# Segment scan of the second block: the key–value update in one round, the output weight held in TensorE, the q feature on VectorE, and a new order on four engines

## The reference

```python
def step(carry, inp):                      # one segment of 32 tokens, all sequences and heads
    mem, z = carry
    q_s, k_s, v_s, qn_s, kn_s = inp        # q, k with rotary embedding; qn, kn without
    scores = jnp.einsum('bhnd,bhmd->bhnm', q_s, k_s) * SCALE
    scores = jnp.where(mask, scores, -jnp.inf)
    sdpa = jnp.einsum('bhnm,bhmd->bhnd', jax.nn.softmax(scores, axis=-1), v_s)
    sq = elu1(qn_s)                        # elu(x) + 1
    num = jnp.einsum('bhnk,bhkv->bhnv', sq, mem)
    den = jnp.einsum('bhnk,bhk->bhn', sq, z)[..., None]
    out = beta * num / (den + 1e-06) + (1.0 - beta) * sdpa
    sk = elu1(kn_s)
    prev_v = jnp.einsum('bhnk,bhkv->bhnv', sk, mem) / jnp.einsum('bhnk,bhk->bhn', sk, z)[..., None]
    mem = mem + jnp.einsum('bhnk,bhnv->bhkv', sk, v_s - prev_v)
    z = z + sk.sum(axis=2)
    return ((mem, z), out)
...
out = o @ w_out                            # o: 16 heads of 64, w_out 1024 x 128; plus the fp8 linear layer of x
```

## Time and profile before

| | |
|---|---|
| median of 3 runs | 3249.21 us (3244.59 to 3251.42) |
| the profiled execution | 3244.0 us |
| its span in the trace | 3242.3 us |
| the scan's first projection to the end | about 1785 to 3242 us |
| PE, DVE, ACT, POOL busy over the span | 86%, 77%, 59%, 58% |

### The profile page before, as it was taken

The page is one execution under the profiler, slowest core; times in us unless marked ns, Lnnn a source line. Parts: engine busy times, 40 slices in busy tenths (PEclk is TensorE's granted clock), DMA queues, the critical chain, the costliest instruction groups (busy, mean ns, idle before and its releaser), DMA issues. The chain is left out here.

```text
span 3242.3 us, 132427 instructions
## 1 busy us (share of the span) xinstructions
PE 2791.2 (86%) x55025; PEld 1639.4 (51%) x55025; DVE 2481.5 (77%) x7469; ACT 1921.3 (59%) x3909; POOL 1895.3 (58%) x2112
## 2 busy tenths in 40 slices
PE   5675999999999999974250899999999999999998
PEld 2332333333333333354130567766676677776666
DVE  3566888888888888856715687887888788778876
ACT  4565788888888888831000555555555555555543
POOL 4664122222222222231053899989999999999986
PEclk9877899999999999986565899999999999999999
DMA  3557433333433334175023000000000000000000
GB/s 112 192 184 240 97 92 98 91 89 94 100 93 91 92 93 102 38 238 149 0 41 87 10 11 11 11 7 8 11 11 11 11 11 11 11 11 11 4 7 11
DMA packets 179276, 210.15 MB, mean 65 GB/s; under 512 B 28592, under 2 KB 140144, under 8 KB 178416
## 3 DMA queue, kind: packets, MB, share of 16 engines
q1 hardware_dynamic: 176112, 200.25, 22.5%
q0 software_dynamic: 2560, 1.35, 0.4%
HBM read 125.10 MB, written 75.63 MB: 62 GB/s over the span
## 5 line engine op out<-in xcount | busy, mean ns | idle before, releaser
L792 ACT ACTIVATE at_pA<-at_ps 128x512 f32<-128x512 f32 x1024 | 562.2, 604 | 47.0 <-DVE at_ps L845 46.0
L845 DVE TENSOR_TENSOR at_ps<-at_ps,w_ratio 128x128 f32<-128x128 f32 (+3 forms) x1024 | 470.7, 494 | 126.7 <-PE at_ps L689 126.2
L664 POOL TENSOR_SCALAR_AFFINE_SELECT at_pB<-at_pB 128x128 f32<-128x128 f32 x256 | 74.8, 292 | 747.4 <-ACT at_pB L798 747.4
L854 DVE CUSTOM_DVE_ANT_0 at_junk<-at_ps,w_cmask 128x512 f32<-128x512 f32 (+3 forms) x1024 | 459.6, 486 | 1.4 <-PE at_ps L702 0.3
L2122 ACT ACTIVATE sc_ee<-sc_ps 128x512 f32<-128x512 f32 x256 | 153.1, 598 | 496.0 <-PE sc_ps L1978 494.7
L798 ACT ACTIVATE at_pB<-at_ps 128x512 f32<-128x512 f32 (+1 forms) x768 | 376.8, 529 | 106.6 <-PE at_ps L702 103.4
L689 PE MATMUL at_ps<-at_aq,at_ak 72*128 72x512 bf16 x1024 | 336.1, 390 | 40.5 <-DMA at_ak<-parts_scratch 35.8
L1942 POOL TENSOR_TENSOR sc_rb<-sc_rb,v_sin 128x512 f32<-128x512 f32 x256 | 326.3, 1275 | 48.6 <-DVE sc_ra L2166 47.8
L1978 PE MATMUL sc_ps<-sc_xT,v_wqkv 128*128 128x512 f32 x512 | 290.4, 650 | 18.9 <-DVE sc_ra L2166 16.7
L689 PEld LDWEIGHTS at_ps<-at_aq,at_ak 72*128 72x128 bf16 x1024 | 100.7, 98 | 400.6 <-DVE at_mx L854 112.7
L722 PE MATMUL at_ps<-at_pA,at_v 128*32 128x512 f32 x2048 | 275.9, 611 | 0.0
(11 more groups left out here) (313 smaller groups left out, 6265.9 us busy)
## 6 DMA issues: line engine op xcount, KB each, us to landing
parts_scratch<-fr_parts SPq DMA_DIRECT2D x64, 384.0 KB, 4.1
at_bq<-parts_scratch SPq DMA_DIRECT2D x192, 96.0 KB
at_bk<-parts_scratch SPq DMA_DIRECT2D x192, 96.0 KB
at_aq<-parts_scratch SPq DMA_DIRECT2D x192, 96.0 KB
at_ak<-parts_scratch SPq DMA_DIRECT2D x192, 96.0 KB
v_scratch<-fr_v SPq DMA_DIRECT2D x32, 352.0 KB, 4.2
at_v<-v_scratch SPq DMA_DIRECT2D x32, 352.0 KB, 3.5
parts_scratch<-fr_parts SPq DMA_DIRECT2D x32, 256.0 KB, 3.9
```

The source lines that it names most:

```text
L792: act.activation(pA[:, n % A_RING, j * S:(j + 1) * S], src, ACT.Exp).then_inc(exped, 1)
L845: dve.tensor_tensor(src[:, 0:wide], src[:, 0:wide], W["ratio"][:, S - wide:S], ALU.mult).then_inc(tilted, 1)
L854: ins = dve.tensor_tensor_reduce(junk[:, P * j * (j + 1) // 2:P * (j + 1) * (j + 2) // 2], src[:, col:col + wide], W["cmask"][:, S - wide: ...
```

## The change

Everything is in `scan`. Line numbers of the changed kernel differ by a few from those above.

1. **Update in one round.** `update` on PE is one block of 32 matmuls instead of two of 16. It writes banks 2 to 5, one per sequence f, with f as the innermost loop. It is done one step later (unit s - 4), and the loop has one more step (133).
2. **Held output weight.** `project_out` is one matmul 128x512 with `v_wout` as the weights and `sc_oT` as the moving operand. The result is turned the other way round, so after eight units ScalarE copies it to a new tile `sc_yT` and PE turns it back (`turn_y`) before VectorE adds it.
3. **q feature on VectorE.** ScalarE makes relu(x) for k alone. POOL's `sigma` runs for k alone. For q, VectorE computes max(x + 1, exp(...)) in one SCALAR_TENSOR_TENSOR that reads x from PSUM.
4. **New orders** of the blocks on PE, ACT, DVE and POOL, with waits named anew. The bank of q is free for k's projection only when VectorE's new instruction has read it.

```diff
-        ee, relu = sb("ee", [P, 2, S]), sb("relu", [P, 2, S])
+        ee, relu = sb("ee", [P, 2, S]), sb("relu", [P, S])
...
-        oT = sb("oT", [P, 2, S])
+        oT, yT = sb("oT", [P, 2, S]), sb("yT", [P, S])
...
-        STEPS = PT + 4
+        STEPS = PT + 5
...
-                    user(("q", s), "rp", 2 * s + 1)
+                    user(("q", s), "sgq", s + 1)
...
-                    def update(p, fs):
+                    def update(p):
                         for g in range(BG):
-                            for f in fs:
-                                for hh in range(2):
-                                    ins = pe.matmul(ps[64 * hh:64 * hh + 64, 4 + f % 2, g * VE:(g + 1) * VE],
+                            for hh in range(2):
+                                for f in range(B1):
+                                    ins = pe.matmul(ps[64 * hh:64 * hh + 64, 2 + f, g * VE:(g + 1) * VE],
                                                     skN[32 * f:32 * f + 32, p % 4, g, 64 * hh:64 * hh + 64],
                                                     uu[32 * f:32 * f + 32, p % PAIRS, g, hh, :], start=True, stop=True)
...
+                    def project_out(p):
+                        wait(pe, "otc", p + 1)
+                        wait(pe, "yt_c", p // PAIRS)
                         h = p % PAIRS
...
+                        pe.matmul(ps[:, 7, :], V["wout"][:, h], oT[:, p % 2], start=(h == 0), stop=(h == PAIRS - 1)).then_inc(G["oproj"], 1)
+
+                    def turn_y(bank, j):
+                        wait(pe, "yt_c", j + 1)
+                        for g in range(BG):
+                            ins = pe.transpose(ps[:, bank, g * P:(g + 1) * P], yT[:, g * P:(g + 1) * P], V["ident"][:])
+                        ins.then_inc(G["yt"], 1)
...
+                        p = s - 4
+                        if inside(p):
+                            wait(pe, "qd", min(s - 1, PT))
+                            wait(pe, "sx", min(s, PT))
+                            wait(pe, "mu", 2 * p)
                             wait(pe, "ud", p + 1)
                             wait(pe, "skc", p + 1)
...
+                            update(p)
...
-                        act.activation(ee[:, n % 2], x, ACT.Relu, scale=-1.0)
-                        act.activation(relu[:, n % 2], x, ACT.Relu).then_inc(G["ex"], 1)
+                        wait(act, ("sgq", "sgk")[which], p)
+                        ins = act.activation(ee[:, which], x, ACT.Relu, scale=-1.0)
+                        if which == 1:
+                            ins = act.activation(relu[:], x, ACT.Relu)
+                        ins.then_inc(G["ex"], 1)
...
+                    def sigma_q(p):
+                        wait(dve, "mn", 2 * p + 1)
+                        wait(dve, "qr_s", p - 3)
+
+                        dve.scalar_tensor_tensor(sig[0][:, p % 4], ps[:, bank_of("q", p), :], 1.0, ee[:, 0], ALU.add, ALU.max).then_inc(G["sgq"], 1)
```

More of the change, by code:

```diff
@@ L1970, in _ @@
                             add_bias(pool, j)
+                        p = s - 2
+                        if inside(p):
+                            wait(pool, "qd", p + 1)
+                            wait(pool, "old", p + 1)
+                            o = ol[:, p % 4].rearrange("p g h d -> p (g h d)")
+                            pool.tensor_tensor(o, o, t2[:, p % 2].rearrange("p c d -> p (c d)"), ALU.add).then_inc(G["od"], 1)
                 @block.tensor
@@ L2035, in turn_keys @@
                     def turn_keys(p):
-                        wait(pe, "sg", 2 * p + 2)
-                        wait(pe, "old", p)
                         for g in range(BG):
@@ L2065, in _ @@
                         if inside(p):
-                            wait(pe, "sg", 2 * p + 2)
+                            wait(pe, "otc", min(s - 3, PT))
+                            wait(pe, "pt", p + 1)
                             wait(pe, "v_c", p + 1)
-                            wait(pe, "qd", p)
+                            local(p)
+                        if s < PT:
+                            values(s)
+                        p = s - 2
+                        if inside(p):
+                            wait(pe, "mu", 2 * min(s - 5, PT - 1) + 1)
+                            wait(pe, "sgk", p + 1)
@@ L2080, in _ @@
-                        if inside(s - 1):
-                            score(s - 1)
+                            wait(pe, "old", min(s - 1, PT))
+                            wait(pe, "sgk", p + 1)
+                            turn_keys(p)
+                        p = s - 1
+                        if inside(p):
+                            wait(pe, "mu", 2 * min(s - 5, PT - 1) + 2)
+                            wait(pe, "add_d", 2 * p + 2)
+                            score(p)
                         if s < PT:
@@ L2142, in _ @@
                             act.activation(ss[:, p % 2], ss[:, p % 2], ACT.Exp).then_inc(G["se"], 1)
[L2143 to L2145 removed]
+                        if s < PT:
+                            features(2 * s + 1)
+                        p = s - 4
+                        if inside(p) and p % PAIRS == PAIRS - 1:
+                            wait(act, "oproj", p + 1)
+                            wait(act, "yt", p // PAIRS)
+                            act.copy(yT[:], ps[:, 7, :]).then_inc(G["yt_c"], 1)
                         p = s - 3
@@ L2201, in _ @@
                             dve.tensor_tensor(by_head(ss[:, p % 2]), scored, bc(head(mx[:]), SEG), ALU.subtract).then_inc(G["sx"], 1)
+                        for j in at_step(s, 1):
+                            moments(dve, link, j)
+                        for j in at_step(s, 2):
+                            shifts(dve, j)
+                        for j in at_step(s, 5):
+                            round_fp8(dve, link, j)
                         p = s - 2
@@ L2221, in _ @@
                             dve.reciprocal(s_, s_).then_inc(G["pt"], 1)
-                        p = s - 3
-                        if inside(p):
-                            update(p, 1)
-                        for j in at_step(s, 1):
-                            moments(dve, link, j)
-                        for j in at_step(s, 2):
-                            shifts(dve, j)
-                        for j in at_step(s, 5):
-                            round_fp8(dve, link, j)
                         if s - 7 in starts:
```

148 lines of the change are left out of this document (67 added, 81 removed).

## The result

| | kernel before | changed kernel |
|---|---|---|
| median | 3246.9 us (4 runs, 3238.3 to 3251.4) | 3213.2 us (4 runs, 3203.8 to 3222.3) |
| ratio, 95% interval | | 0.990 [0.986, 0.994] |
| fourteen rounds of eight steps, each | 89.9 us | 87.9 us |

The changed kernel is 34 us faster. The profiled execution took 3222.3 us, the longest of the four.

What follows compares the result with a forecast made beforehand. PE (83.8) and POOL (82.4) bound the 89.7 us period, with waiting between them. New PE floor 79.6, stalls 3.3 and coupling 1.5 gave 84.4; sixteen rounds saved 85 from 3244.0, plus 2 tail and 5.2 for runs: 3166 us, range 3130 to 3226.

Steps and rivals of the forecast that it cites:

- coupling: Time engines lose waiting for one another in the scan: estimated 1.5 us per eight steps, bounds 0 and 4.5.
- PE's floor: PE's summed block times per eight scan steps without waits: 83.8 us before, forecast 79.6 after.
- period: Time of eight scan steps: 89.7 us before, forecast 84.4 after, 5.3 less.
- dense step: PE's scan step without the recall of q's 0.42 us wait: 10.27 us before, forecast 9.68 after.
- rival B: PE's update keeps its rate because loads or PSUM writes bind: period 88.0, total 3224 us; chance 0.20.
- The rounding's stall: Rounding before the division for q stalls PE at the update 3.0 us per segment: 4.34 long, 1.35 hidden.
- The tail: After the last matmul, a copy, turn_y and two memory additions come before the last addition: 2 us more.
- Rival D: VectorE keeps 2.15 us idle per step, so eight steps take 94.5 us and the total 3328; chance 0.09.
- Rival C: The rounding's stall is mostly absorbed and little coupling is left: period about 81, total 3112 us; chance 0.09.

Runs made afterwards that it cites:

- supply runs: Two kernels with the scan replaced by score-form matmuls alone, 384 pairs per step, no waits or other engines: fp32 3305.1 us, bf16 3316.3 us.
- more instructions: Changed kernel with both projections and the output projection each cut into four matmuls of 128 columns: 3259.0 us, 1.006 of the kernel before.
- update's order: Changed kernel with the update's matmuls in the old order, sequences 0 and 1 for all groups, then 2 and 3, still one block: 3206.8 us, 0.991.
- both: Changed kernel with the mask added by two matmuls instead of eight and rotated q and k stored as bf16 for the scores: 3148.2 us, 0.972.
- rounding at the end: Changed kernel with the fp8 rounding moved back to the end of VectorE's step, behind the memory additions: 3250.1 us, 1.004.
- both, rounding parted: Changed kernel with two mask matmuls, bf16 scores, and the rounding split, two instructions before the division for q and two after: 3155.1 us, 0.973.
- before, PE alone: PE's list of the kernel before, run on constants without waits or other engines, update halves writing four banks: 84.9 us per round.
- changed, PE alone: PE's list of the changed kernel, run in its order on constants without waits or the scan's other engines: 83.0 us per round.

## Why the prediction was off

**The step that failed** is the last line of the sum, "To this comes coupling ... I take 1.5 (an estimate, from that comparison; bounds 0 and 4.5)". I had read the 5.9 us between PE's floor and the period as waiting of the engines for one another, and concluded that it shrinks when POOL's load falls. PE's own breaks for want of instructions had no place in the sum. Taken the same way after the change (period 87.9, blocks 78.7, stall at the rounding some 1.2), the term is 8.0. Of this, 4.3 are breaks in PE's list that the list has when alone; the other 3.7 are further breaks and waits for VectorE, mixed. 22 blocks of 256 instructions at the 3.75 us of the supply runs are 82.5 us, close to the 83.0 measured alone. A PE floor of 79.6, as I forecast, was below that and could not be reached.

The traces allow a plainer split. No block of matmuls has a semaphore wait in its middle, so idle time of PE there is its own; idle time ahead of a block may be a wait. Us per round over thirteen rounds of each trace, from the start and end of every matmul, gaps over 0.08 us:

| kernel | round | idle inside blocks | idle ahead of blocks |
|---|---|---|---|
| before | 89.9 | 2.2 | 1.5 |
| changed | 88.0 | 5.4 | 1.3 |
| more instructions | 91.0 | 7.0 | 1.4 |
| update's order | 87.7 | 4.2 | 1.4 |
| mask in two matmuls | 86.9 | 4.6 | 2.1 |
| bf16 scores | 84.5 | 2.9 | 3.4 |
| both | 83.8 | 1.4 | 4.7 |
| rounding at the end | 90.7 | 4.7 | 3.6 |
| both, rounding parted | 84.5 | 1.6 | 4.8 |
| q feature on POOL | 90.1 | 4.5 | 3.5 |
| before, mask in two | 88.6 | 1.6 | 1.6 |
| before, PE alone | 84.9 | 0.8 | 0 |
| changed, PE alone | 83.0 | 3.2 | 0 |

From before to changed the waits ahead of blocks stayed, and the breaks inside blocks grew by 3.2: there is the time that came back. They grow with instructions added and shrink with instructions taken away or with longer work, and as they shrink the waits grow: both theories have a share. With the rounding at the end and with the q feature on POOL, where POOL works beside the rounding, it is the waits that grew. Why the changed kernel's breaks are 5.4 inside the kernel and 3.2 alone stays open.

A sign of it was in my own rows: the recall of q in the earlier trace rows has 54 of 64 matmuls in its row. I called its missing 0.42 "a wait" and took it out of the dense step, though a block has no wait in its middle. The 97.1 us of "issue" that the earlier trace rows give the recall's weight loads point the same way but can't be read as breaks: PE's own breaks at L1994 are 15.5 us.

Point by point:

- *Update in one round*, 0.80 forecast: 0.84 measured. Its rate does follow the order of the tiles, as 0.99 for the other order shows, so rival B is out, and with it the rule that weight loads bind here: their mean is still 130 ns. But the gain is one of PE time, and the kernel with the other order shows how little such time is worth here.
- *Output projection*, 1.05 forecast: 0.96.
- *q feature*, 745 ns forecast: 678 ns. POOL per round 72.2 forecast: 72.4. DVE 77.4 forecast: 74.6, of which the shorter rounding makes 1.9.
- *The rounding's stall*, 3.0 forecast: 1.15 in the step shown (14.5 in 17 waits over the fourteen rounds). The mechanism was right (its length less the 1.35 that I had found hidden), the length was mis-sized: 2.46 and not 4.34. It is 1.9 us per round to the good, 30 us in all, and hid part of the other miss. That was luck: I had taken the length where POOL was at work and didn't ask whether it would be at the new place.
- *The period*: 84.4 forecast, 87.9 measured. The fall was 2.0 instead of 5.3; times sixteen, the 3.3 us between make 53 us, and the miss is 47. By terms: PE's floor 0.9 lower, the stalls 2.1 lower, the coupling 6.5 higher, 3.5 in all.
- *The tail*, 2 us more forecast: from the end of the fourteenth round to the end of the span it is 112.8 before and 114.8 after.
- *Rival D* (VectorE keeps its idle time, 3328): DVE does wait in several places per step, but it is idle for 1.7 us per step and not 2.15, and the period did not grow. *Rival C* wanted the stall mostly absorbed and little coupling; the first came true in part (1.15 us, where 3.0 was forecast), the second didn't.

Neither the held output weight nor the one-round update was tried alone on the kernel before. And why a block takes 3.75 us on the mean with a spread from 3.3 to over 4, while its packet takes 0.9 to 1.5, stays open.

## What to carry to other kernels

Count PE's instructions, not only its time: where a stretch of small matmuls comes near 3.75 us per 256 instructions (loads and matmuls both, fp32 twice), fewer instructions make it faster, by wider tiles or by bf16, and time saved inside the blocks turns for the most part into "issue". Look for idle time in the middle of a block, where no semaphore can be the cause. Run an engine's list alone, without waits, before an idle time is put down to the other engines. And price an instruction on VectorE with its neighbour on GpSimd in view: the same rounding cost 2.5 or 4.3 us, and a faster kernel moved POOL back beside it.

## What the runs showed of the hardware

- PE's instructions come in packets of 16 KB, and a list of small matmuls alone got one in 3.75 us on the mean, with fp32 and bf16, at a granted clock of 0.50 (1.2 GHz); the mixed list alone at 1.00 (2.4 GHz) got one in 3.77 us, 22 in 83.0. The Trainium skill ("Runtime: NRT & Kernel Launch", Instruction fetch mechanics) has the 16 KiB blocks of 256 instructions, which the packets bear out, and calls the cost of crossing a boundary mostly hidden. That doesn't hold here: 1.9 to 2.5 us of 3.75 were open in the runs with scores alone, and 0.4 to 0.5 us per step in the changed kernel's list alone. The measurement decides.
- The rate of matmuls on 32 x 64 weight tiles depends on the order in which the tiles follow: 64 of them took 0.84, 0.99 or (two halves apart from each other, two banks each) 1.25 us.
- VectorE's TENSOR_SCALAR and TENSOR_TENSOR on SBUF took 0.43 and 0.69 us alone and 1.37 and 1.63 beside a GpSimd instruction.
- PE's granted clock was 0.50 in the two runs whose scan had PE idle for 53 and 60 of 90 us, and also in the one with one moving column per matmul, where its rows show PE busy for 82.0 of 84.0; it was 1.00 in the scans of before and after and in both lists alone.
